# A first stage reordered: conditioning loads on another queue, a matrix series among the steps of a basis correction

## What is computed

```
ada = silu(cond) @ W_ada + b_ada          # 4 x 3456: six sections of 576
shift_msa, scale_msa, gate_msa, shift_mlp, scale_mlp, gate_mlp = split(ada, 6)
h = layernorm(x) * (1 + scale_msa) + shift_msa
x = x + gate_msa * attention(h, W_qkv, b_qkv, W_proj, b_proj)      # 16 heads of 36
h = layernorm(x) * (1 + scale_mlp) + shift_mlp
x = x + gate_mlp * (gelu(h @ W_fc1 + b_fc1) @ W_fc2 + b_fc2)
U, _ = qr(P)                              # P is 576 x 64
v = silu(cond) @ W.T + b                  # 4 x 2016: the upper triangle of A
R = expm(A)                               # A skew, 64 x 64 for each of the 4
out = x + (x @ U @ R - x @ U) @ U.T
```

## Time and profile before

| | |
|---|---|
| three runs | 3201.93, 3202.49, 3209.22 us; median 3202.49 |
| the profiled execution | 3204.2 us, span 3202.5 us |
| TensorE matmul busy | 2868.2 us, 90% of the span |
| VectorE, ScalarE, GpSimd busy | 1638.2, 1457.6, 1438.2 us |
| `stage_prepare` | 0 to 176.7 us of the span |

### The profile page before, as it was taken

One profiled execution on the slowest core, in us unless ns is written; L12 is line 12 of the kernel. 1 busy time (PEld: TensorE's weight loads), 2 busy tenths in 40 slices (PEclk: granted clock), 3 DMA queues, 4 the chain that ended last, 5 costly groups with the idle time before them and its releaser, 6 DMA issues. The chain is left out here.

```text
span 3202.5 us, 49786 instructions
## 1 busy us (share of the span) xinstructions
PE 2868.2 (90%) x16066; PEld 2278.3 (71%) x16066; DVE 1638.2 (51%) x2847; ACT 1457.6 (46%) x1863; POOL 1438.2 (45%) x1065
## 2 busy tenths in 40 slices
PE   6859999979999999999999677869999999999976
PEld 3147878856666666666566466759999999999965
DVE  3446666558888888888888546501111111111125
ACT  2112222238888898888888635521111111111112
POOL 1233332128888888888888735422222222222200
PEclk9869999979999999999999878879999999999988
DMA  5466665653334333333333267693211211211153
GB/s 172 139 217 219 226 221 206 230 142 78 89 80 91 77 90 81 86 90 79 91 78 90 75 179 217 201 303 113 71 36 36 71 36 36 71 36 36 51 152 140
DMA packets 340330, 378.72 MB, mean 118 GB/s; under 512 B 167008, under 2 KB 230120, under 8 KB 340188
## 3 DMA queue, kind: packets, MB, share of 16 engines
q1 hardware_dynamic: 328494, 354.69, 37.2%
q0 software_dynamic: 4224, 9.44, 1.6%
q10 hardware_dynamic: 7474, 12.68, 1.3%
HBM read 226.82 MB, written 158.93 MB: 120 GB/s over the span
## 5 line engine op out<-in xcount | busy, mean ns | idle before, releaser
L811 POOL TENSOR_TENSOR a_pl<-a_pf,a_ph 128x1024 fp32r<-128x1024 f32 x384 | 913.5, 2399 | 46.7 <-ACT a_pf L899 46.2
L834 DVE TENSOR_REDUCE a_mx<-a_psum_s 128x1 f32<-128x1024 f32 x496 | 606.4, 1223 | 177.3 <-PE a_psum_s L910 169.2
L897 ACT ACTIVATE a_ph<-a_psum_t 128x1024 fp32r<-128x1024 f32 x512 | 526.2, 1028 | 143.5 <-PE a_psum_t L942 125.4
L1545 PE MATMUL m_psum_h<-m_ht,m_w 128*128 128x256 f32 x4032 | 534.5, 284 | 30.9 <-DMA m_w<-w_s 21.9
L1497 POOL TENSOR_TENSOR m_al<-m_af,m_ah 128x256 fp32r<-128x256 f32 x288 | 213.1, 740 | 763.2 <-DVE m_ah L1506 763.2
L1545 PEld LDWEIGHTS m_psum_h<-m_ht,m_w 128*128 128x128 f32 x4032 | 508.9, 190 | 34.2 <-issue 34.2
L1506 DVE CAST m_ah<-m_af 128x256 fp32r<-128x256 f32 x288 | 84.6, 294 | 849.0 <-ACT m_af L1483 849.0
L1483 ACT ACTIVATE m_af<-m_psum_h,m_bias 128x256 f32<-128x256 f32 x288 | 137.0, 476 | 815.1 <-PE m_psum_h L1545 815.1
L1559 PE MATMUL m_psum_y<-m_w,m_ah 128*128 128x288 f32 x2304 | 504.9, 296 | 1.4 <-DVE m_y L1523 1.2
L961 PE MATMUL a_psum_o<-a_ph,a_vs 128*100 128x512 f32 x1024 | 405.7, 396 | 3.7 <-POOL a_pl L811 3.6
L962 PE MATMUL a_psum_o<-a_pl,a_vs 128*100 128x512 f32 x1024 | 404.2, 395 | 0.0
(11 more groups left out here) (222 smaller groups left out, 3097.6 us busy)
## 6 DMA issues: line engine op xcount, KB each, us to landing
a_qs<-q_s SPq DMA_DIRECT2D x192, 144.0 KB
a_ks<-k_s SPq DMA_DIRECT2D x192, 144.0 KB
w_s<-q_ws SPq DMA_DIRECT2D x64, 324.0 KB, 3.5
h_s<-p_ht SPq DMA_DIRECT2D x40, 512.0 KB, 5.2
m_ht<-h_s SPq DMA_DIRECT2D x16, 1280.0 KB, 8.4
v_s<-q_vo SPq DMA_DIRECT2D x64, 288.0 KB, 2.3
a_vs<-v_s SPq DMA_DIRECT2D x128, 144.0 KB, 4.5
q_s<-q_qko SPq DMA_DIRECT2D x32, 512.0 KB, 2.9
```

Of the source, the lines that this page charges most:

```text
L811: pool.tensor_tensor(pl[:, s % RING], pf[:, s % RING], raw(ph[:, s % RING]), ALU.subtract).then_inc(lo_pool, 1)
L834: dve.tensor_reduce(mx[:, u % 2, t:t + 1], p_s[:], AX.X, ALU.max).then_inc(s_free, 1)
L897: act.activation(ph[:, s % RING], p_t[:, s % 2], ACT.Exp, scale=SCALE)
L1545: m = pe.matmul(p_h[:, f % RING, 0:GM], w1[:, k, f * P:(f + 1) * P], ht[:, q, a], start=(i == 0), stop=(i == len(PASSES) - 1))
```

## The change

SP's queue now loads the three `wa` tiles and `b_fc2`, behind P and ahead of the weight blocks, so ACT's queue holds four issues ahead of Silu. VectorE copies `m` and `pt` first and the conditioning after them. The `a` tiles are taken in the order 0, 1, 2, 4, 5, 6, 3, 7, so that the six that hold the modulation sections come first; GpSimd makes the modulation rows once those six are there, and the bias product last. Rows of `up` are issued alternately: 31 by ACT behind the first four `a` tiles, 32 by SP ahead of its last three weight stores. The transposes of `up` and of the modulation rows stand directly behind the 64 steps, and the three rounds of the series between the steps of the basis correction. SP stores `mod` first of the three results.

```diff
-        PE_STEPS = ("gram", "p_turned", "l_turned", "q_ready", "q_turned", "gram2", "fix", "top", "a_turned") \
-            + tuple(f"taylor{i}" for i in range(1, TERMS))
+        PE_STEPS = ("gram", "p_turned", "a_turned", "l_turned", "taylor1", "q_ready", "taylor2", "q_turned", "gram2",
+                    "fix", "taylor3", "top")
...
-        fill += [("a", n, k) for n in range(NT) for k in range(NK)]
+        fill += [("a", n, k) for n in A_ORDER for k in range(NK)]
+        MOD_TILES = 6
+        UP_TILES = 4
...
+        def load_wa(eng, i):
+            n = A_ORDER[i]
+            cols = slice(n * WT, (n + 1) * WT)
+            s = i % A_RING
+            eng.dma_start(wa[:, s, 0:FULL], w_ada[0:FULL * P, cols].rearrange("(k p) n -> p k n", p=P)) \
+               .then_inc(wa_in[s], 16)
+            eng.dma_start(wa[0:REM, s, FULL], w_ada[FULL * P:C, cols]).then_inc(wa_in[s], 16)
+            eng.dma_start(wa[REM:REM + 1, s, FULL], b_ada[cols].rearrange("(a n) -> a n", a=1)) \
+               .then_inc(wa_in[s], 16)
+
+        def load_up(eng, r):
+            off = r * (R - 1) - r * (r - 1) // 2
+            eng.dma_start(up[r:r + 1, :, r + 1:R], v[:, off:off + R - 1 - r],
+                          allow_slow_non_contiguous=True).then_inc(up_in, 16)
...
+                for i in range(A_RING):
+                    load_wa(sp, i)
+                sp.dma_start(bb[:], row(b_fc2).broadcast_to([B, C])).then_inc(b_in, 16)
                 for j in range(RING):
                     sp.dma_start(wf[:, j], blocks[j][0]).then_inc(wf_in[j], 16)
                 for j, (_, dst) in enumerate(blocks):
+                    if j == NV - 1:
+                        sp.wait_ge(masks, 5)
+                        sp.wait_ge(v_done, NV)
+                        for r in range(0, R - 1, 2):
+                            load_up(sp, r)
                     sp.wait_ge(w_lo, j + 1)
...
+                sp.wait_ge(mt_ready, 1)
+                sp.dma_start(mod.rearrange("b p n -> p b n"), mt[:]).then_inc(out_done, 16)
                 sp.wait_ge(bias_gated, 1)
...
-                for n in range(A_RING):
-                    load_wa(n)
-                act.dma_start(bb[:], row(b_fc2).broadcast_to([B, C])).then_inc(b_in, 16)
                 act.wait_ge(c_in, 16)
                 act.activation(cs[:, 1], cs[:, 0], ACT.Silu).then_inc(silu_done, 1)
...
-                pool.wait_ge(v_done, NV + NT)
-                pool.wait_ge(b_in, 16)
-                pool.tensor_tensor(av[:, GB_FC2 * C:(GB_FC2 + 1) * C], av[:, GATE_MLP * C:(GATE_MLP + 1) * C], bb[:],
-                                   ALU.mult).then_inc(bias_gated, 1)
+                pool.wait_ge(v_done, NV + MOD_TILES)
                 for i, s in enumerate(MOD):
...
+                        if 0 <= place < UP_TILES:
+                            for r in range(place * R // UP_TILES + 1, min((place + 1) * R // UP_TILES, R - 1), 2):
+                                load_up(act, r)
```

More of the change, by code:

```diff
@@ L1833, in stage_prepare @@
             fill += [("v", h - 1, k) for k in range(NK)] if h else []
-        fill += [("a", n, k) for n in range(NT) for k in range(NK)]
+        fill += [("a", n, k) for n in A_ORDER for k in range(NK)]
+        MOD_TILES = 6
+        UP_TILES = 4
+        assert all(n in A_ORDER[:MOD_TILES] for s in MOD for n in range(s * C // WT, ((s + 1) * C - 1) // WT + 1))
+        def load_wa(eng, i):
[11 more added lines that the diff above has]
+                          allow_slow_non_contiguous=True).then_inc(up_in, 16)
         with nc.Block() as block:
@@ L1937, in _ @@
                         act.activation(dst, p_v[0:B, i % 2, 0:w], ACT.Copy).then_inc(v_done, 1)
[L1938 to L1947, removed]
+                        place = i - NV
+                        if place >= 0 and place + A_RING < NT:
+                            load_wa(act, place + A_RING)
+                        if place == 0:
+                            act.wait_ge(masks, 5)
+                            act.wait_ge(v_done, NV)
+                        if 0 <= place < UP_TILES:
+                            for r in range(place * R // UP_TILES + 1, min((place + 1) * R // UP_TILES, R - 1), 2):
+                                load_up(act, r)
                         if block_no < len(blocks):
@@ L1972, in _ @@
                 dve.wait_ge(set_up, 3)
[L1973 to L1978, removed]
                 dve.wait_ge(pe_done, pe_at("gram"))
@@ L2095, in _, with taylor @@
                 i.then_inc(c_turned, 1)
+                def taylor(t):
+                    pe.wait_ge(dve_done, dve_at(f"y{t - 1}"))
+                    for b in range(B):
+                        for s in range(2):
+                            i = pe.matmul(p_s[:, b, s, 0:R], sa[:, b, 1 - s], ex[:, b, s], start=True, stop=True)
+                    step(i, f"taylor{t}")
                 pe.wait_ge(dve_done, dve_at("pt"))
                 pe.wait_ge(sct_ready, 2)
-                pe.wait_ge(set_up, 4)
+                pe.wait_ge(set_up, 5)
                 for j in range(R):
@@ L2104, in _ @@
                         filling(*f)
+                pe.wait_ge(up_in, 16 * (R - 1))
+                for b in range(B):
+                    i = pe.transpose(p_s[:, b, 0, 0:R], up[:, b], ident[0:R, 0:R])
+                step(i, "a_turned")
+                pe.wait_ge(v_done, NV + MOD_TILES + 1)
+                pe.wait_ge(am_ready, 2 * len(MOD))
+                for i in range(len(MOD)):
+                    for k in range(NK):
+                        t = pe.transpose(p_m[:, i * NK + k], am[:, i, k * P:(k + 1) * P], ident[0:B, 0:B])
+                t.then_inc(m_turned, 1)
                 pe.wait_ge(dve_done, dve_at("scaled"))
                 step(pe.transpose(p_g[0:R, 0:R], sq[:], ident[0:R, 0:R]), "l_turned")
+                taylor(1)
                 pe.wait_ge(dve_done, dve_at("lst"))
@@ L2110, in _ @@
                 step(i, "q_ready")
+                taylor(2)
                 pe.wait_ge(dve_done, dve_at("qt"))
```

78 lines of the change are left out of this document (35 added, 43 removed).

## The result

The changed kernel takes **3176.14 us** (median of five runs, 3174.54 to 3184.91) against 3203.53 (five runs, 3201.93 to 3212.2) for the kernel before: ratio 0.9915, 95% interval 0.9902 to 0.9928. The profiled execution took 3176.74 us, its span is 3175.1 where it was 3202.5: 27.4 us less. The first stage ends at 151.5 us instead of 176.7, which is 25.2 of the 27.4.

What follows compares the result with a forecast made beforehand. The first stage, serial behind a barrier, was taken to pass its savings whole to the end: -10.9 + 0 + 2.7 - 10.0 = -18.2 us, 3186.0 for the profiled execution, forecast median 3184.3, range 3177 to 3195.

Steps and rivals of the forecast that it cites:

- (1): Start of first stage: weight issues leave ACT's queue, Silu runs early, first basis step at 12.35 not 23.29; -10.9 us.
- (2): Basis steps: new filling order and skew-matrix row copies split between ACT and SP change nothing; 0, bounds -1 and +1.
- (3): Basis steps: GpSimd's eight modulation instructions among them make VectorE wait 0.7 us in about four steps; +2.7 us.
- The 0.50 us: Query stage: a VectorE instruction beside GpSimd scaling took 0.50 us, 0.29 more; nearest row for pricing modulation rows among basis steps.
- TensorE's level: Basis steps: the phase at which TensorE's clock falls may shift them some 5 us either way; nothing in the sum.
- (4): Tail of first stage: series rounds between correction steps, no store on the path, 21.15 against 31.16; -10.0 us, bounds -12 and -7.5.
- The 13.7: Tail: basis correction with the series rounds between its steps, summed as 10.2 + 2.0 + 1.5 us.
- TensorE is at the low level in the first nine steps: Rival, first basis steps: TensorE warm from the first step, gaining about 4 us more, 3180; chance 0.06.
- Silu is early: Rival, start: Silu still late because its input lands behind large transfers, 3192.3 to 3195.2 us; chance 0.06.
- GpSimd's rows hold next to nothing: Rival, basis steps: GpSimd holds every step it meets, all 7.84 us lost or TensorE slowed, 3189 to 3193; chance 0.10.
- the series does join the correction: Rival, tail: series products wait for late skew-row copies, so the tail's gain halves, 3189 us; chance 0.04.
- The clock eats it: Rival, basis steps: more steps fall to TensorE's low level, 0.84 us each; 22 more use up the gain; chance 0.04.

Runs made afterwards that it cites:

- the three kernels on the other chip: Changed kernel with series rounds back behind the basis correction, 3183.57 us; with GpSimd's modulation rows and transposes late, 3183.67; with sixteen extra GpSimd scalings, 3180.17.
- the kernel before with the pair apart: Kernel before, with a basis step's reciprocal written to PSUM and its scale taking m and neg as per-partition scalars: 3188.31 us, ratio 0.9957.

## Why the prediction was right or wrong

(1) **Start: right.** Forecast 12.35 for the first step, measured 12.04; -11.3 instead of -10.9. SP's longer queue delayed nothing: the first of its blocks (the prediction calls them projection weights; they are the query weights) was read at 34.30, as forecast.

(2) **Filling order and rows split: 0, and it holds only because the rows were split.** With the start gained and the rows left on ACT, 2.0 to 2.4 us of it go into the tail (two runs). I read that ACT's late evacuations held nobody in the trace of before. They did not hold TensorE, but the last one already stood behind the row issues and the root behind it, 1.31 us from the end of the steps where it is 0.76 now; with the steps early the rows reach further.

(3) **GpSimd's rows among the steps: +2.7 forecast, +0.46 measured.** The step that failed is the one that let every such instruction hold the step it meets for its mean rest, 0.7 us, as if a scaling held for its whole 1.6 us. It holds for its first 0.46 us. With that window a step that arrives at random waits 0.46 x 0.46 / (2 x 1.96) = 0.05 us on average, and the six steps that meet the rows some 0.3 together (an estimate from these rows). The 0.50 us was near the upper size of a hold and not its mean. The Trainium skill ("SBUF — State Buffer", "Who interferes with whom") says a VectorE instruction with two inputs in SBUF contends with a GpSimd instruction that reads SBUF. The trace agrees for two-tensor products, to their whole length as the prediction has it from the same section: every held scale ends with the product. For these scalings it agrees that they contend (0.67 us) and not that it is for their whole length (0.46 us of 1.64). The same page of the Trainium skill says that an instruction with at most one SBUF input doesn't contend, outside what it calls the 2-port perf modes. The 276 to 278 ns of the update above agree; line 2018 with its 1.29 us would have to be the exception, and no profile shows its mode.

**TensorE's level: not a term, measured -4.0 us.** This is the second step that failed, and the larger: I had the level as a spread of 5 either way that adds nothing to the sum. The 64 steps became 2.9 us shorter where I had them 2.7 longer. Steps 46 to 49 gave 4.0 us; a hold at step 42 that is 0.40 us longer, and 0.39 more in the step behind it, took 0.8 back, and the rows 0.5. So beside the rows the steps changed by -3.3. That -4.0 came and not +4.0 is luck as far as the prediction goes. What the runs show of it: in each of the eleven profiles with holds there are 7 to 17 low steps, and most spells lie behind holds (steps 14 to 17, 22 to 25, 31 to 35, 44 to 49, with the holds at 13, 21, 29, 33, 42 and 45); in the two with neither holds nor the wait for `c_wa` there is one; and a 3.12 us pause put there by another cause is followed by three. A hold alone doesn't make a spell: behind the one at step 29, 2.8 us long, the next three steps are high in both profiles of each kernel. What is open is what decides how many steps a spell lasts: the one that begins at step 44 lasts six in the kernel before and two in the change. Each half of the change alone ends it early at step 46, and so does the reordering of the first copies alone; other kernels with a like start lengthen other spells. I could not forecast it from this trace, and a better range would have been wider downwards.

(4) **Tail: -10.0 forecast, -11.1 measured,** inside its bounds. To the basis product 6.1 against 6.7, correction with rounds 13.1 against 13.7, barrier 0.8 against 0.75. The 13.7 was added up wrongly: its last term, 1.5, should have been 1.24 + 0.5 = 1.74 by its own rows. The hold of the copies by GpSimd's product came (line 2018, 1.29 us beside 1.40). The root ended at 134.24 and VectorE was free for its reciprocal only at 135.05, so the hold cost some 0.7 us and not 0.3, and the last evacuation, 0.55 earlier, won most of it back; the first series product added 1.2 and not 1.7.

Of the 9.2 us missed, 0.35 belong to the start, 2.2 to GpSimd's rows, 3.3 to the clock less the longer hold, 1.1 to the tail and 2.2 to later stages, where no run tells them from the spread of one kernel. The rivals: TensorE is at the low level in the first nine steps as before (0.65 to 0.69 us); Silu is early; GpSimd's rows hold next to nothing; the series does join the correction. "The clock eats it" had the right place and the other sign. Its price was real: five low steps more went with 4.5 us more in the steps with the rows on ACT, and 15 instead of 7 with 2.6 to 5.1 us in the three kernels on the other chip.

## What to carry to other kernels

A chain of small dependent steps pays for a hold twice, once in the wait and once in the slower matmuls behind it: here 14 us of holds and, by the kernel before with the pair apart, some 9 of clock, together about what the start and the tail were worth, and it stood in the trace of before as six rows of 1.85 to 2.83 us that I used only as a bound. Look for such rows and take the operand pair apart first. And when a chain is made shorter, ask of every queue beside it whether its issues now end after it: here ACT's row copies, which cost half a microsecond before, became what the next step waited for in five trial kernels. To price one engine's instruction beside another's, look at where in it the other one started and when it was let go, over several rows, and not at one length.

## What the runs showed of the hardware that I had not expected

A VectorE instruction that takes its tensor from PSUM and two per-partition scalars from SBUF is not held at all (0.268 to 0.272 us in 192 instructions of three kernels, 36 of them beside GpSimd's large products), while the same arithmetic with two SBUF tensors lasts up to 2.89 us; it costs 0.06 us more than the 0.21 when nothing is beside it. How long a GpSimd instruction holds such a pair is not simply its own length: one with two tensors (128x1296) holds to its end, 2.92 us, and one with a single tensor (4x576) for 0.46 of its 1.64 us. GpSimd's spans are rough in a profile, but both numbers come back within 0.02 us in every run. The same issue of one conditioning tile's rest took 5.17 to 6.79 us in ACT's queue in five profiles, and Silu's table load moved between 18.96 and 20.56 with it. A row copy's issue took about 0.6 us (9 in 5.46), and up to 1.36 in ACT's queue at single places among the steps.
